# Attention's normalized rows split and turned by the transposing DMA, result rows stored in halves, other state-space tables

## What is computed

```python
# 32 batches, 128 state rows + 77 text rows = 205 rows of width 1024
h = ssm(log_dt, Lambda, x, L=1024)          # (32,128,1024): sum over 64 complex modes of W * exp(P)
h = concatenate([h, txt], axis=1)           # (32,205,1024)
n = layernorm(h)
q, k, v = n @ wq, n @ wk, n @ wv            # 32 query heads, 8 key/value heads of 32 columns
attn = softmax(causal(q @ k.T * 32**-0.5))
h = h + (attn @ v) @ wo
h = h + layernorm(h) @ W.T + b              # W: base plus a masked low-rank update in a Fourier basis
```

## Time and profile before

| | |
|---|---|
| median of 3 runs | 3081.81 us (3081.46 to 3085.93) |
| the profiled execution | 3082.04 us, its span 3080.3 us |
| PE busy | 2781.2 us, 90% of the span |
| DVE, ACT, POOL busy | 1997.8 (65%), 1094.1 (36%), 1029.9 us (33%) |
| mean granted TensorE clock | 0.965 |
| `ssm` and weight preparation | about 0 to 229 us |
| `attention` | about 229 to 1890 us |
| `prep_out`, then `output` | 1890 to 2010, 2010 to 3080 us |

### The profile page before, as it was taken

The page is one execution under the profiler, slowest core; times in us unless marked ns, Lnnn a source line. Parts: engine busy times, 40 slices in busy tenths (PEclk is TensorE's granted clock), DMA queues, the critical chain, the costliest instruction groups (busy, mean ns, idle before and its releaser), DMA issues. The chain is left out here.

```text
span 3080.3 us, 70678 instructions
## 1 busy us (share of the span) xinstructions
PE 2781.2 (90%) x27970; PEld 2030.8 (66%) x28224; DVE 1997.8 (65%) x4642; ACT 1094.1 (36%) x2362; POOL 1029.9 (33%) x1402
## 2 busy tenths in 40 slices
PE   0847799999999999999999986699999999999999
PEld 0736698989899898989898883244444444444444
DVE  8874577787787878777787865444444444444443
ACT  3331355555555555555555565211001101100110
POOL 4631254544545454554445454011101110110110
PEclk9977899999999999999999996599999999999999
DMA  5642422222222322222222223154554455455453
GB/s 179 194 116 69 103 58 78 58 75 78 57 76 60 80 58 77 69 65 77 56 76 58 69 49 144 55 122 120 129 137 123 121 133 132 118 127 137 124 122 86
DMA packets 446040, 297.32 MB, mean 97 GB/s; under 512 B 389416, under 2 KB 407976, under 8 KB 445232
## 3 DMA queue, kind: packets, MB, share of 16 engines
q1 hardware_dynamic: 445472, 282.69, 35.7%
q10 hardware_dynamic: 240, 10.09, 1.1%
HBM read 116.36 MB, written 80.61 MB: 64 GB/s over the span
## 5 line engine op out<-in xcount | busy, mean ns | idle before, releaser
L693 POOL TENSOR_SCALAR_AFFINE_SELECT p<-p 128x256 f32<-128x256 f32 (+1 forms) x768 | 334.3, 437 | 762.0 <-ACT p L720 743.6
L805 DVE TENSOR_REDUCE mx<-psS 77x2 f32<-77x410 f32 (+1 forms) x768 | 449.3, 613 | 181.9 <-PE psS L912 110.7
L930 PE MATMUL psJ<-xth,qh 128*128 128x205 f16 x2048 | 522.0, 255 | 24.9 <-DVE qsl L813 24.7
L932 PE MATMUL psJ<-xth,ql 128*128 128x205 f16 x2048 | 518.4, 253 | 0.0
L931 PE MATMUL psJ<-xtl,qh 128*128 128x205 f16 x2048 | 516.5, 252 | 0.0
L720 ACT ACTIVATE p<-psT,escale 128x410 f32<-128x410 f32 (+1 forms) x768 | 410.4, 570 | 276.2 <-PE psT L870 256.8
L698 POOL TENSOR_TENSOR pl<-p,ph 128x410 f16<-128x410 f32 (+1 forms) x512 | 447.7, 894 | 102.5 <-ACT ph L727 95.7
L1257 POOL TENSOR_TENSOR hb<-h,bias_sb 128x1024 f32<-128x1024 f32 x52 | 122.5, 2355 | 962.4 <-DVE h L1293 962.4
L1271 ACT CAST xh<-xn 128x1024 f16<-128x1024 f32 x52 | 54.4, 1045 | 967.1 <-DVE xn L1302 967.1
L1332 PE MATMUL ps5O<-woh,ath 128*128 128x512 f16 x832 | 316.2, 380 | 26.3 <-DMA atl<-al 26.3
L1293 DVE SCALAR_TENSOR_TENSOR h<-ps5O,osc,h_in 128x512 f32<-128x512 f32 x104 | 78.1, 751 | 402.4 <-PE ps5O L1334 402.4
(11 more groups left out here) (227 smaller groups left out, 5906.9 us busy)
## 6 DMA issues: line engine op xcount, KB each, us to landing
a_in<-acat SPq DMA_DIRECT2D x52, 512.0 KB, 3.8
h_in<-hcat SPq DMA_DIRECT2D x52, 512.0 KB, 4.7
qst<-qsh SPq DMA_DIRECT2D x512, 51.2 KB, 2.1
out<-y SPq DMA_DIRECT2D x51, 512.0 KB, 3.1
hcat<-ob SPq DMA_DIRECT2D x64, 256.0 KB, 4.0
xin<-hcat SPq DMA_DIRECT2D x32, 512.0 KB
acat<-ao SPq DMA_DIRECT2D x32, 512.0 KB
qst<-qsl SPq DMA_DIRECT2D x256, 51.2 KB, 2.1
```

The lines of the kernel that those rows point to most:

```text
L693: pool.affine_select(out=v, in_=v, compare_op=ALU.is_ge, fill=0.0, base=0, pattern=[[0, v.shape[1]], [1, w]], channel_multiplier=-1).then_ ...
L805: dve.tensor_reduce(dst, v, AX.X, ALU.max).then_inc(s_read, 1)
L930: pe.matmul(ps[:, 0:S], wh[:, k, c], xth[:, par, k, :], start=k == 0, stop=False)
L932: m = pe.matmul(ps[:, 0:S], wl[:, k, c], xth[:, par, k, :], start=False, stop=k == KC - 1)
```

## The change

In `ssm`: the four rounded phases become two, found by two fused VectorE operations each; the four sine tables are made from them by ScalarE with absolute values and shifted arguments; the exponentials `size` and `ela` are made directly by 36 small ScalarE activations; all four products with `size` go to VectorE; the partial sum of `es` is gone and TensorE does 16 matmuls a chunk.

In `attention`: the x units are gone. In slot 3 VectorE only negates the mean. In slots 4 and 5 ScalarE, behind its copies of the slot's units, subtracts the mean of one row tile in place and scales it to the float16 high part (`high_part`), VectorE makes the low part behind the slot's `pl` and ahead of `norm` (`low_part`), and SP, as the last thing of a step, turns both parts with DMA transposes (`turn`, four a step). TensorE waits for them at the start of the next step. Loads and stores of rows go to ScalarE's queue, at the start of slots 2 and 6; a store is of half the columns. `norm` has one reciprocal and one product. SP restacks the first half of k ahead of the first half of q.

```diff
@@ units @@
-                if s >= 4 and has["ln"]:
-                    row.append(("x", s - 4))
@@ attention, SP @@
-                if has["load"]:
-                    wait(sp, pj_filled, base)
-                    load(b + 4, par)
...
-                if has["last"]:
-                    store(b - 1, nxt)
                 if has["qkv"]:
 
+                    wait(sp, pj_lo, base + at(rows, "k", 0) + 1)
+                    wait(sp, st_filled, 24 * b + 12)
+                    restack(K_PARTS, kst[par], slice(0, 1), k_in[0])
                     wait(sp, pj_lo, base + at(rows, "q", 3) + 1)
-                    wait(sp, st_filled, 24 * b + 12)
                     restack(Q_PARTS, qst[par], HALVES[0], q_in[0])
                 if has["max"]:
                     wait(sp, pj_lo, base + at(rows, "m", 0) + 1)
                     shift_rows(0, nxt)
-                if has["qkv"]:
-                    wait(sp, pj_lo, base + at(rows, "k", 0) + 1)
-                    restack(K_PARTS, kst[par], slice(0, 1), k_in[0])
+                if has["ln"]:
+                    wait(sp, pj_filled, base)
+                    for t in range(2):
+                        turn(t, nxt, b + 3)
...
+            def turn(t, to, n):
+                r, cols = ((P, slice(0, P)), (TROWS, slice(P, P + TROWS)))[t]
+                sp.wait_ge(x_hi, 2 * n + t + 1)
+                sp.dma_start_transpose(out=xth[:, to, :, cols], in_=xfh[0:r, t, :]).then_inc(xt_in[to], 16)
+                sp.wait_ge(x_lo, 2 * n + t + 1)
+                sp.dma_start_transpose(out=xtl[:, to, :, cols], in_=xfl[0:r, t, :]).then_inc(xt_in[to], 16)
@@ attention, GpSimd @@
+            pool.memset(xfh[:, 1, :], 0.0)
+            pool.memset(xfl[:, 1, :], 0.0)
@@ attention, ScalarE @@
+            def store(b, half):
+                c = slice(half * D // 2, (half + 1) * D // 2)
+                act.wait_ge(norm_done, 8 * b + 4 * half + 4)
+                act.dma_start(acat[b * S:b * S + P, c], ao[:, half, 0, :]).then_inc(a_out[half], 16)
+                act.dma_start(acat[b * S + P:b * S + S, c], ao[0:TXT, half, 1, :]).then_inc(a_out[half], 16)
+
+            def high_part(b, par, t):
+                r, x = T[t], xin[0:T[t], 1 - par, t, :]
+                if t == 0:
+                    act.wait_ge(ln_done, b + 4)
+                    if b >= -2:
+                        act.wait_ge(xt_in[par], 64 * ((b + 2) // 2 + 1))
+                act.activation(x, x, ACT.Identity, bias=nmean[0:r, t:t + 1]).then_inc(centred, 1)
+                act.wait_ge(centred, 2 * (b + 3) + t + 1)
+                act.activation(xfh[0:r, t, :], x, ACT.Copy, scale=rs[0:r, 3, t:t + 1]).then_inc(x_hi, 1)
...
                 for g in SLOTS:
+                    if g == 2 and has["load"]:
+                        wait(act, x_lo, 2 * (b + 3))
+                        load(b + 4, par)
+                    if g == 2 and has["last"]:
+                        store(b - 1, 1)
+                    if g == 6 and has["att"]:
+                        store(b, 0)
                     if has["att"]:
                         for k in range(3):
...
                         n += 1
+                    if g in (4, 5) and has["ln"]:
+                        high_part(b, par, g - 4)
@@ attention, VectorE @@
-                dve.reciprocal(rden[:, 0, :], o[:, 0, :, HD]).then_inc(rec_done, 1)
-                dve.reciprocal(rden[0:TXT, 1, :], o[0:TXT, 1, :, HD]).then_inc(rec_done, 1)
...
+                dve.reciprocal(rden[:], o[:, :, :, HD]).then_inc(rec_done, 1)
...
-                    for t in range(2):
-                        r = T[t]
-                        dve.tensor_scalar(x[0:r, t, :], x[0:r, t, :], mv[0:r, t, 0:1],
-                                          rs[0:r, 3, t:t + 1], ALU.subtract, ALU.mult).then_inc(ln_done, 1)
+                elif g == 3:
+                    dve.tensor_scalar(nmean[:], mv[:, :, 0], -1.0, None, ALU.mult).then_inc(ln_done, 1)
+
+            def low_part(b, par, t):
+                r = T[t]
+                dve.wait_ge(x_hi, 2 * (b + 3) + t + 1)
+                dve.scalar_tensor_tensor(xfl[0:r, t, :], xin[0:r, 1 - par, t, :], rs[0:r, 3, t:t + 1], xfh[0:r, t, :],
+                                         ALU.mult, ALU.subtract).then_inc(x_lo, 1)
...
                     if has["ln"] and g < 4:
                         layer_norm(b, par, g)
+                    if has["ln"] and g in (4, 5):
+                        low_part(b, par, g - 4)
                     if has["att"] and g:
                         norm(b, par, g - 1)
@@ attention, TensorE @@
+                if has["qkv"]:
+                    pe.wait_ge(xt_in[par], 64 * ((b + 2) // 2 + 1))
@@ ssm, GpSimd @@
-            for k in range(2):
-                pool.tensor_tensor(size[:, k], per_row(a[:]), per_step(iqr[:, k, :]), ALU.mult).then_inc(size_arg, 1)
...
-                pool.tensor_tensor(tab[:, t], tab[:, t], size[:, 0], ALU.mult).then_inc(tab_ab, 1)
@@ ssm, ScalarE @@
+            for k in range(2):
+                for r in range(LR):
+                    m = act.activation(size[:, k, :, r], a[:], ACT.Exp, scale=iqr[:, k, r:r + 1])
+                m.then_inc(size_ok, 1)
...
+            act.activation(turned[:, 1], turned[:, 0], ACT.Abs, scale=-1.0, bias=phase[:, 0:1]).then_inc(far_ok, 1)
+            act.activation(tab[:, 1], turned[:, 0], ACT.Sin, scale=-TWO_PI, bias=lag[:, 0:1]).then_inc(sine_ok, 1)
@@ ssm, VectorE @@
-            for t in range(4):
-                dve.wait_ge(turned_ok, t + 1)
-                chain(dve.tensor_scalar(tab[:, t], turned[:, t], ROUND, ROUND, ALU.add, ALU.subtract))
-                dve.tensor_tensor(turned[:, t], turned[:, t], tab[:, t], ALU.subtract).then_inc(frac_ok, 1)
+            chain(dve.tensor_scalar(tab[:, 0], base, phase[:, 0:1], ROUND, ALU.add, ALU.add))
+            dve.scalar_tensor_tensor(turned[:, 0], tab[:, 0], ROUND, base, ALU.subtract,
+                                     ALU.subtract).then_inc(frac_ok, 1)
...
-                dve.tensor_tensor(es[:, ch % 2, 0, 0:SUMMED], es[:, ch % 2, 0, 0:SUMMED],
-                                  es[:, ch % 2, 1, 0:SUMMED], ALU.add).then_inc(e_ok, 1)
@@ ssm, TensorE @@
-                    last = 0 if j < SUMMED else 1
-                    for k in range(last + 1):
+                    for k in range(2):
```

More of the change, by code:

```diff
@@ L205, in _ @@
             act.activation(dt[:], ldt[:], ACT.Exp).then_inc(dt_ok, 1)
+            act.wait_ge(ab_ok, 1)
+            for k in range(2):
+                for r in range(LR):
+                    m = act.activation(size[:, k, :, r], a[:], ACT.Exp, scale=iqr[:, k, r:r + 1])
+                m.then_inc(size_ok, 1)
+            for la in range(LA):
+                m = act.activation(ela[:, la, :], a[:], ACT.Exp, scale=ila[:, la:la + 1])
+            m.then_inc(la_exp_ok, 1)
             act.wait_ge(args_ok, 1)
@@ L252, in _ @@
             chain = Chain(dve, dve_c)
-            for t, (top, bottom) in enumerate(((0.25, 0.25), (0.5, 0.0), (0.25, 0.0), (0.0, 0.25))):
-                dve.memset(phase[0:N, t:t + 1], top)
-                m = dve.memset(phase[N:P, t:t + 1], bottom)
+            for half, back in ((slice(0, N), 0.0), (slice(N, P), -0.25)):
+                dve.memset(phase[half], back)
+                dve.memset(lag[half], back * TWO_PI)
+            m = dve.memset(quarter[:], 0.25 * TWO_PI)
             chain(m)
@@ L274, in _ @@
             chain(dve.tensor_scalar(f[:], b[:], tp, None, ALU.mult))
-            for k in range(2):
-                dve.tensor_tensor(bases[k], per_row(f[:]), per_step(iqr[:, k, :]), ALU.mult).then_inc(base_ok, 1)
             for k, src in enumerate((a, b)):
@@ L376, in _ @@
                         pe.wait_ge(k_read, n - 3)
-                    last = 0 if j < SUMMED else 1
-                    for k in range(last + 1):
+                    for k in range(2):
                         m = pe.matmul(ps[n % 4][:, j % 2, :], u[:, ch % 2, j].rearrange("p a c -> p (a c)"),
-                                      es[:, ch % 2, k, j, :], start=k == 0, stop=k == last)
+                                      es[:, ch % 2, k, j, :], start=k == 0, stop=k == 1)
                     if j % 2:
@@ L456, in attention @@
     T = (P, TXT)
+    TROWS = 80
     with ExitStack() as ctx:
@@ L781, in layer_norm @@
                     rsqrt(dve, chain, rs, mv[:, :, 1])
-                else:
-                    chain.n = 18
-                    for t in range(2):
-                        r = T[t]
-                        dve.tensor_scalar(x[0:r, t, :], x[0:r, t, :], mv[0:r, t, 0:1],
-                                          rs[0:r, 3, t:t + 1], ALU.subtract, ALU.mult).then_inc(ln_done, 1)
-                    dve.sem_inc(dve_ln, 2)
+                elif g == 3:
[5 more added lines that the diff above has]
+                                         ALU.mult, ALU.subtract).then_inc(x_lo, 1)
             def take_maxes(b, j, base, ks, late_read):
@@ L929, in unit @@
```

(10 more changed lines are left out.)

118 lines of the change are left out of this document (54 added, 64 removed).

## The result

The changed kernel takes **3272.45 us** (median of 4 runs, 3271.80 to 3274.41); the kernel before took 3081.64 us beside it. The ratio is 1.0636, with a 95% interval from 1.0585 to 1.0687: slower by 6.4%. The prediction was 3215 us with a range from 3140 to 3285. The profiled execution has a span of 3272.7 us at a mean granted TensorE clock of 0.935, where it had 3080.3 us and 0.965.

What follows compares the result with a forecast made beforehand. TensorE's instruction list was taken to set a step's length. From 3082 us: +122 (29 steps of +4.2), +10 clock, +15 before step 0, +4 last steps, -18 state-space tables = 3215 us, range 3140 to 3285.

Steps and rivals of the forecast that it cites:

- the stall ahead of q5: Slot 4 into 5: TensorE waits for q4's low part, 4.0 us a step, between 3.4 and 5.0.
- Slots 5 and 6: Slot 6: TensorE waits 0.7 us behind ScalarE's exponential and 1.7 for the third maxima tile; slots 4 to 7 take 24.5.
- The gains: Steady attention: removed x units, the wait ahead of ("m", 0) and k's wait save 2.5 us a step.
- The clock: Steady attention: TensorE's clock falls behind the 4.0 us stall in one step in seven, +10 us, bounds 0 and 73.
- the clock falls in each step: Rival, 12%: the 4 us stall lowers TensorE's clock as the 4.78 us one did, giving 3278 us.
- the likeliest case: The whole kernel at 3215 us, with its own range of 3160 to 3270 and a 70% chance.
- Slot 2: Four row DMA issues on ScalarE ahead of slot 2's exponentials cost +0.5 us a step, 0 to 1.3.
- Before step 0: Ahead of attention's step 0: waits for transposes that SP issues last cost +15 us, 5 to 22.
- State-space tables: In ssm: the first matmul comes near 61 us, saving 18 us (5 to 25); the loop changes by 0.
- Last steps and output: End of the kernel: the last steps pay the DMA issues, +4 us, 0 to 8.
- the other engines keep pace: Rival, 8%: engines beside TensorE hold nothing up, only the removed TensorE work shows, giving 2996 us.
- the turned rows land late: Rival, 10%: SP's transposes finish after the next step begins, 1.5 us a step likely, giving 3258 us.

Runs made afterwards that it cites:

- late low parts: The changed kernel with VectorE making the low parts of the normalized rows in slots 5 and 6 instead of 4 and 5: 3132.77 us.
- single pass: The changed kernel without ScalarE's pass that subtracts the mean, so rows are scaled but not centred: 3144.44 us.
- the filler: The changed kernel with slot 5's second raw-score tile computed 14 times instead of once, to keep TensorE busy while it would wait: 3231.29 us.
- kernel without x units and with k first: The kernel before with the new state-space part, merged normalization, k restacked ahead of q, and x units only for the first two batches: 2980.91 us.
- the two small edits: Normalization in two operations and k restacked ahead of q, run on the kernel before together with the new state-space part: 3047.11 us.
- kernel with SP's DMAs: The changed kernel with loads and stores of rows issued by SP again and none by ScalarE: 3226.79 us.
- gaps: The changed kernel with ScalarE's passes in slots 2 and 3, low parts ending slots 4 and 5, row DMAs in slot 1, later turned-row waits: 3041.35 us.

## Why the prediction was right, and which term was mis-sized

**The bound and the mechanism held.** TensorE's list sets the step and the stall ahead of q5 is where the change loses. Its chain had been worked out as two passes (2.2 us), `low_part` (1.2), `norm` (0.65) and the copy (0.36) behind ("m", 0). Measured: 2.31, 1.28, 0.57 and 0.36, and a stall of 3.77 us for 4.0. The late low parts (140 us back) and the single pass (113 us back in the steps) show that this is the cause. VectorE's wait for ScalarE's scaled rows became its largest between 400 and 1780 us, 163.1 us in 48 waits, as the last part had said.

**Slots 5 and 6.** 1.77 us for the third maxima tile of slot 6 was predicted as 1.7. The wait of slot 6's score tile, predicted as 0.7, is 0.43 with the filler and at most 0.21 in three steps of the change. The four slots were predicted at 24.5 us; with the clock up, in the kernel with the filler, they take 24.5.

**The gains.** The kernel without x units and with k first gives 2.3 us a step for them, the two small edits 18 / 29 = 0.6: 2.9 together, where the sum had 2.5.

**The clock: the term that was mis-sized.** The prediction took "one step in seven: +10 us". The clock falls in every step, often twice, and the filler shows that it costs 2.1 us a step in length, 29 x 2.1 = 61 us. The bound that was written beside it, 29 x 2.5 = 73, holds that cost; the loss itself is larger, 3.3 us a step. In words: the outcome of 3272 lies nearest to the rival "the clock falls in each step" (3278), which had 12%, and not in the middle of the likeliest case (3215, own range to 3270). The stated range held the time only because that rival had set its top; without it the 51 us missing from this term would have been a miss. The flaw is in the step from the rows to the chance. A wait of 4.78 us was followed by half speed, and the steady stalls of 0.8 us by none; 4.0 lies close to the first, and I took it as though it lay in between. It also counted one fall a step. Where there is a second, it comes directly on the first or behind the 1.77 us wait of slot 6.

**Slot 2.** Predicted +0.5. The wait for ScalarE there is 0.97 us, and the way from slot 2 to q3 takes 9.62 us for 8.56: +1.1. The four issues took 2.0 us, inside the 1.7 to 2.7; it was the wait ahead of q3 that didn't absorb its share, it is still 0.66 us for 0.72. The kernel with SP's DMAs gives the same price, 1.0 us a step with slot 6's issues in it.

**Before step 0.** The first dense scores of step 0 begin at 346.4 in both kernels, but the first projection came 7 us earlier (243.8 for 250.9) and `ssm` ended 13.4 earlier: +13.4 us, predicted +15.

**State-space tables.** First matmul at 63.09, predicted near 61: the rounding ended at 27.00 as predicted, but each table product takes 3.97 us beside GpSimd and not 3.4. The loop was predicted at 0 and costs 3.2. Together -13.4 for -18.

**Last steps and output.** +4 predicted; the span's growth leaves about 1. Output takes 1084.3 us in both, from its first matmul.

**The sum again.** 3082 + 29 x 4.5 (stalls, less the gains) + 29 x 2.1 (clock) + 13 - 13 + 1 = 3274, against 3274 of the profiled execution (span 3272.7 and what lies around it). It has to close, since 4.5 and 2.1 are two parts of the measured step; what it shows is their shares. The same sum had 122 and 10 in place of 130 and 61.

**The rivals.** That the other engines keep pace (2996) is refuted: the order held, not the load. That the turned rows land late is refuted for the change, and becomes true when its steps are shortened (late low parts: 39.2 us in 26 waits; gaps: 13.0 in 14).

**Left open.** How long a stall must be for the clock to fall isn't settled by these runs: over the same 1380 us it fell in 4 places where the longest stall was 2.5 us, in 17 where it was 2.7 and in 17 where it was 3.2, and in every step where it was 3.8, but also in 17 where 1.8 was the longest and stood close behind a shorter one, and in one in the kernel before, whose longest is 1.8 too. The same two waits left it up in one step and not in the step before. Why the clock of `prep_out` differs between profiled executions is open as well. Why the version in the gaps is 46 us above its expectation is told by its steps and waits only, not by a run.

## What to carry to other kernels

When work moves off the bounding engine, ask of each instruction that it adds elsewhere what stands behind it in its queue: here one VectorE instruction that waited for ScalarE stood ahead of the low part that frees TensorE's bank, and that cost more than all the matmuls it replaced; one slot later, three quarters of the loss were gone. A stall of TensorE that comes back in each step is to be priced twice, once as time and once as a chance near one of a lowered clock behind it, when it is anywhere near a stall that lowered it before. And removed work on the bounding engine is worth nothing while the next list in line, SP's restacks here, ends at the same time: move that first, then remove. And before a difference of 20 us is put down to an edit, look at the clock in the parts that the edit doesn't touch.

## What the hardware showed that I had not expected

- Matmuls that compute nothing new made the kernel 41 us faster (3231.29 for 3272.45), because TensorE's clock stayed at full speed behind the stall of slot 5.
- Each fall of the clock in steady attention looks the same: about 3.4 us at 1.2 GHz, 1.7 us of full-speed time lost; in some steps two directly on each other, 3.4 lost. Behind the 4.78 us wait it was 5 us at half speed. The Trainium skill, TensorE: Matmul & The Clock Gate, section HAM oscillation — how this bites in real kernels, tells of a kernel whose every tile waited and whose every tile then began slowly; the changed kernel's 36 places in 24.5 steps agree with it.
- Four plain DMA issues cost ScalarE 0.34 to 0.63 us each; the engine stood for 2.01 us.
- A VectorE product of 128 x 2048 float32 took 3.97 us beside GpSimd's work (15.90 for four), where an operation of that size with two inputs took 2.29 us at 21.33, when GpSimd hadn't begun.
- `prep_out` ran its 32 products at about half speed in nine of the eleven profiled executions (0.53 in the changed kernel) and at full speed in two, though its code is the same in all: 44.5 us against 25.1.
